# One transformer tower layer on one core: convolution taps from PSUM, a first chain in halves, and a reordered start of the selective scan

## What is computed

```
proj = x @ in_proj.T;  hidden, gate = split(proj)           # 384 channels each
h  = silu(causal_conv4(hidden) + conv_b)                    # depthwise, 4 taps
ts, B, C = split(h @ x_proj.T)                              # 48, 16, 16
dt = softplus(ts @ dt_proj.T + dt_b); dt[last] *= alpha
state = exp(A*dt)*state + dt*B*h;  y = sum_n state*C        # 16 states a channel
out = ((y + h*D) * silu(gate)) @ out_proj.T
```

## Time and profile before

| | us |
|---|---|
| median of three runs (lowest, highest) | 377.47 (377.18, 379.12) |
| the profiled execution, its own time | 380.98 |
| span in its profile | 378.0 |
| TensorE, VectorE, ScalarE, GpSimd busy | 331.5, 243.0, 195.2, 205.5 |

### The profile page before, as it was taken

The page is one execution under the profiler, slowest core; times in us unless marked ns, Lnnn a source line. Parts: engine busy times, 40 slices in busy tenths (PEclk is TensorE's granted clock), DMA queues, the critical chain, the costliest instruction groups (busy, mean ns, idle before and its releaser), DMA issues.

```text
span 378.0 us, 6192 instructions
## 1 busy us (share of the span) xinstructions
PE 331.5 (88%) x1980; PEld 271.4 (72%) x1981; DVE 243.0 (64%) x372; ACT 195.2 (52%) x321; POOL 205.5 (54%) x160
## 2 busy tenths in 40 slices
PE   4898667999987998999798959999999999999960
PEld 3753256867866975688687848888888888888850
DVE  0469789689999899899997966853333222223210
ACT  0126676496994675686925697723233333333310
POOL 2143039898899998898866157500233333333333
PEclk9999855899996799999789696999999999999995
DMA  7990470000023410310999996232233322333222
GB/s 193 273 280 0 148 300 2 0 0 6 2 89 134 151 73 9 105 42 2 195 207 244 290 225 219 86 68 65 53 51 49 49 49 49 49 49 49 21 22 21
DMA packets 30183, 37.00 MB, mean 98 GB/s; under 512 B 6112, under 2 KB 26128, under 8 KB 29136
## 3 DMA queue, kind: packets, MB, share of 16 engines
q1 hardware_dynamic: 23536, 30.54, 29.4%
q0 software_dynamic: 4080, 4.39, 7.7%
q10 hardware_dynamic: 2544, 1.77, 1.9%
HBM read 28.29 MB, written 8.40 MB: 97 GB/s over the span
## 4 chain that ended last, share of the span: by engine, by line
PE 39%; DMA 23%; DVE 15%; issue 11%; ACT 5%; POOL 5%; POOLq 1%; SPq 0%; DVEq 0%; ACTq 0%
DMA out<-ysb,token_r 19%; PE ps L1593 7%; DVE decays L1098 5%; PE ps L1571 5%; POOL states L577 4%; PE ps L1745 3%; PE ps L1427 3%; DMA c_all<-in_xT 3%; PE ps L1432 3%; ACT decays L789 2%; DVE ysb L1319 2%; PE ps L1444 1%; PE ps L1712 1%; DVE xn L974 1%; PE ps L1737 1%
## 5 line engine op out<-in xcount | busy, mean ns | idle before, releaser
L577 POOL TENSOR_TENSOR states<-decays,c_all 128x1024 f32<-128x1024 f32 x48 | 114.2, 2394 | 16.7 <-DVE decays L1098 16.6
L1098 DVE TENSOR_TENSOR_SCAN decays<-decays,ps 128x1024 f32<-128x1024 f32 x48 | 108.1, 2269 | 9.8 <-PE ps L1571 7.3
L679 POOL DMA_INDIRECT out<-ysb,token_r x23 | 36.1, 1570 | 69.1 <-DVE ysb L1319 51.5
L789 ACT ACTIVATE decays<-dt,negA 128x504 f32<-128x504 f32 (+1 forms) x104 | 61.8, 675 | 3.1 <-POOL states L577 3.1
L1593 PE MATMUL ps<-ident,states 128*128 128x128 f32 x384 | 57.3, 296 | 2.5 <-DVE diagB L1021 1.5
L1308 DVE TENSOR_TENSOR hm<-ps,sa 128x512 f32<-128x512 f32 x31 | 21.4, 691 | 55.9 <-PE ps L1718 52.6
L1593 PEld LDWEIGHTS ps<-ident,states 128*128 128x128 f32 x384 | 45.2, 151 | 6.7 <-issue 2.1
L1571 PEld LDWEIGHTS ps<-diagB,stacked_u 64*128 64x128 f32 x384 | 31.8, 207 | 22.1 <-issue 12.6
L1571 PE MATMUL ps<-diagB,stacked_u 64*128 64x128 f32 x384 | 42.3, 318 | 5.9 <-DVE decays L1098 4.6
L901 ACT ACTIVATE sa<-ps 128x512 f32<-128x512 f32 x31 | 18.5, 596 | 55.0 <-PE ps L1718 55.0
L1745 PE MATMUL ps<-w,hT 128*128 (+1 forms) x248 | 45.5, 327 | 0.1
(11 more groups left out here) (195 smaller groups left out, 576.8 us busy)
## 6 DMA issues: line engine op xcount, KB each, us to landing
c_all<-c_scratch SPq DMA_DIRECT2D x8, 1024.0 KB, 4.8
w_raw<-in_w13T SPq DMA_DIRECT2D x9, 512.0 KB, 10.8
w_raw<-in_w13T SPq DMA_DIRECT2D x18, 256.0 KB, 11.3
w<-in_w2T SPq DMA_DIRECT2D x9, 384.0 KB, 15.7
xs<-rows_scratch SPq DMA_DIRECT2D x23, 128.0 KB, 2.4
rows_scratch<-zeros SPq DMA_DIRECT2D x5, 520.0 KB, 6.4
c_all<-in_xT SPq DMA_DIRECT2D x8, 256.0 KB, 10.5
out<-h SPq DMA_DIRECT2D x1, 576.0 KB, 3.5
```

The source lines that it names most:

```text
L577: pool.tensor_tensor(states[:, n % SLOTS, :].rearrange("p (n b s) -> p n b s", n=NH, b=2), decays[:, k % DBUF, t, :, :, :].rearrange("p b ...
L679: pool.indirect_dma_start(out=out_d, out_offset=bass.IndirectOffsetOnAxis(ap=token_r[:, r:r + 1], axis=0), in_=ysb[:, r, :], in_offset=Non ...
L789: return act.activation(decays[:, k % DBUF, tiles[0]:tiles[1], :, n, 1:], dt[g][:, i, tokens].rearrange("p (a b s) -> p a b s", b=2, s=S)[ ...
L1098: dve.tensor_tensor_scan(both, both, unit_banks(n).rearrange("p b n -> p (b n)"), 0.0, ALU.mult, ALU.add).then_inc(scan_ok, 1)
```

## The change

1. Patch products go to six banks (`PATCH_BANK`), so that TensorE waits for VectorE only from tile 6 on; the first transposes come after tile 6 instead of tile 5. VectorE's constants come ahead of the first tile, and the group 1 rows are normalised by ScalarE (`second_rows_normed`, with `less_mean` from GpSimd).
2. `hp` and its zero columns are gone. ScalarE's `projected` writes the projection times the last tap plus the bias into `hid`, and VectorE's `tap` adds the other three taps straight from the PSUM bank, over 63, 62 and 61 columns of each image.
3. Group 1's projections are no longer in front of the scans: `project_first(3)` and `project_second(3)` stand within the first chain, projection 4 after unit 1, projection 5 after units 2 and 3. Their convolutions stand in VectorE's list after scans 0, 3 and 4. A bank is free for the next product when its taps are done (`conv_ok` in place of `hidden_ok`).
4. The chain of z = 0 goes in halves of 256 tokens, from `first_linear` to `first_inputs`, and its copies in `first_copies` by tiles of 128.
5. GpSimd builds `spread_u` and `spread_b` before its first `inverse_deviation`. It builds two diagonals instead of one before the scans, and u for chunk 1 after unit 2.
6. The loads of `outT`, `gateTa` and `gateTb` go from ScalarE's queue to SyncE's, behind the patches.

```
 for n in range(UNITS):                       # VectorE
     scanned(n)
     if n == 0:
-        first_stacked(1)
-        diagonal(0, BUILT_BY_DVE[2])
+        first_low(1)
+        convolved(1, 0)
     if n == 1:
-        u_low_part(1)
+        rest_stacked()
+        diagonal(0, BUILT_BY_DVE[2])
     if n == 2:
+        time_step(0, 1)
         diagonal(0, BUILT_BY_DVE[3])
-    if n == 5:
+    if n == 3:
+        convolved(1, 1)
+    if n == 4:
+        u_low_part(1)
+        convolved(1, 2)
+    if n == 6:
         time_step(0, 2)
...
+def tap(g, i, d):
+    out = hid[g][:, i, :].rearrange("p (b s) -> p b s", b=GB)[:, :, d:]
+    source = ps[:, PROJ_BANK[IC * g + i], :].rearrange("p (b s) -> p b s", b=GB)[:, :, 0:S - d]
+    return dve.scalar_tensor_tensor(out, source, par[:, i, P_CW + K - 1 - d:P_CW + K - d], out,
+                                    ALU.mult, ALU.add)
...
 def projected(n):                            # ScalarE
-        act.activation(hp[:, g, m, :, K - 1:],
-                       ps[:, PROJ_BANK[n], :].rearrange("p (b s) -> p b s", b=GB),
-                       ACT.Copy).then_inc(hidden_ok, 1)
+        act.activation(hid[g][:, m, :], ps[:, PROJ_BANK[n], :], ACT.Identity,
+                       bias=par[:, m, P_CB:P_CB + 1],
+                       scale=par[:, m, P_CW + K - 1:P_CW + K]).then_inc(hidden_ok, 1)
...
-PROJ_BANK = [4, 5, 6, 7, 4, 5, 6, 5, 7, 4, 7, 4]
+PROJ_BANK = [4, 5, 6, 7, 7, 5, 6, 5, 7, 4, 7, 4]
+PATCH_BANK = [0, 1, 4, 5, 6, 7, 0, 1]
...
-PROJ_FREE = {4: 1, 5: 2, 7: 3}
+PROJ_FREE = {3: IC, 4: IC + 1, 5: IC}
...
+            if n in PROJ_FREE:
+                pe.wait_ge(conv_ok, PROJ_FREE[n])
...
 def u_copies(z, half):                       # TensorE
     elif z == 1:
         pe.wait_ge(stacked_ok, 2)
+        pe.wait_ge(conv_ok, G * IC)
...
+def first_copies():
+    pe.wait_ge(half_high, 1)
+    pe.wait_ge(conv_ok, IC)
+    for a in range(2):
+        for low in range(2):
+            if low and a:
+                inputs(0)
+            if low:
+                pe.wait_ge(half_low, 1)
...
-    if n in (1, 10, 21, 25, 34):
-        u_transposes((1, 10, 21, 25, 34).index(n) + 1)
+    if n in (4, 10, 21, 25, 34):
+        u_transposes((4, 10, 21, 25, 34).index(n) + 1)
...
-    if n in (3, 13, 22, 28, 37):
-        u_copies((3, 13, 22, 28, 37).index(n) + 1, 0)
+    if n in (5, 13, 22, 28, 37):
+        u_copies((5, 13, 22, 28, 37).index(n) + 1, 0)
+    if n == 1:
+        project(IC + 1)
     if n == 2:
+        project_first(2 * IC - 1)
+    if n == 3:
+        project_second(2 * IC - 1)
         time_step_product(0, 2)
```

More of the change, by code:

```diff
@@ L629, in _ @@
             pool.tensor_scalar(spread_b[:, :, 128:], source[:, :, 0, :], 0.0, None, ALU.mult).then_inc(copies_ok, 1)
+            for g in range(G):
+                inverse_deviation(pool, chain, g)
             pool.wait_ge(diagonal_ok, 1)
@@ L998, in _ @@
                               0.0, None, ALU.is_gt)
+            dve.wait_ge(ident_ok, 2)
+            dve.tensor_reduce(on_diagonal[:, :], ident[:, :].rearrange("p (q t) -> p t q", t=BLOCK), AX.X,
+                              ALU.add).then_inc(diagonal_ok, 1)
+            dve.wait_ge(ld_pos, 48)
+            chain(dve.tensor_tensor(posb[:, :], posb[:, :], projb[:, :], ALU.add))
+            for t in range(TPG):
+                embedded(t)
+                if t:
+                    statistics(t - 1, h0_ok)
+            moments(0, h0_ok)
+            embedded(TPG)
+            normed(0)
+            for t in range(TPG + 1, TT):
+                embedded(t)
+                statistics(t - 1, h0_ok)
+            moments(1, h0_ok)
             dve.wait_ge(ld_par, 48)
@@ L1513, in u_copies @@
             def u_copies(z, half):
-                if half:
+                if z and half:
                     pe.wait_ge(stacked_ok, 2 * z + 1)
@@ L1532, in u_copies, with first_transposes @@
                                      skip_group_check=True)
[L1533 to L1552 removed]
+                last.then_inc(stack_mm, 1 if z else 2)
+            def first_transposes(half):
+                if half:
+                    pe.wait_ge(u_ok, 1)
+                    pe.wait_ge(first_ok, 1)
+                else:
+                    pe.wait_ge(half_u, 1)
+                for q in range(2):
+                    tokens = slice(HALF * half + 128 * q, HALF * half + 128 * (q + 1))
+                    last = pe.matmul(first_u(half)[:, 128 * q:128 * (q + 1)], u[:, 0, tokens], ident[:, :],
+                                     start=(q == 0), stop=True, is_transpose=True, skip_group_check=True)
+                last.then_inc(uT_mm if half else half_uT, 1)
+            def first_copies():
[7 more added lines that the diff above has]
+                            pe.wait_ge(half_low, 1)
+                        for j in range(BLOCKS):
+                            last = pe.matmul(ps[:, 5 + a, 128 * j:128 * (j + 1)],
+                                             spread_u[:, j, 0:128] if low else spread_u[:, j, 2 * BLOCK:],
+                                             u_low[:, 128 * a:128 * (a + 1)] if low else
+                                             u_high[:, 0, 128 * a:128 * (a + 1)],
+                                             start=(not low and j == 0), stop=True, skip_group_check=True)
+                    last.then_inc(first_mm, 1)
             def inputs(n):
@@ L1576, in inputs @@
                 last.then_inc(dbu_mm, 1)
+            pe.wait_ge(xnT_ok, 2)
+            pe.wait_ge(ld_par, 48)
+            pe.wait_ge(h0_ok, TPG + 1)
+            for n in range(IC):
+                project(n)
+            transposes(1)
+            pe.wait_ge(ld_mid, 32)
+            pe.wait_ge(h0_ok, TT)
+            for i in range(IC):
+                coefficients(0, i)
+            pe.wait_ge(xnT_ok, 2 * G)
+            project_first(3)
+            time_step_product(0, 0)
+            b_transposes(0)
+            project_second(3)
+            b_copies(0)
+            first_transposes(0)
+            first_copies()
+            time_step_product(0, 1)
+            first_transposes(1)
             def summed(n):
```

277 lines of the change are left out of this document (156 added, 121 removed).

## The result

| | before | after |
|---|---|---|
| median, same chip | 378.30 us | 384.92 us |
| ratio, 95% interval | | 1.0174 (1.0117 to 1.0231) |
| the profiled execution, its span | 380.98, 378.0 us | 387.68, 385.9 us |

Slower by 6.6 us; 3.0 were forecast, and 384.9 lies outside the range of 375.2 to 383.0.

What follows compares the result with a forecast made beforehand. VectorE's list of work was taken to pace the scans. Queue waits spend the first scan's lead: unit 16 3.2 us late, less 0.2 regained, is +3.0 on 377.47, giving 380.5 us; range 375.2 to 383.0.

Steps and rivals of the forecast that it cites:

- first scan: End of the halved first chain: the first scan starts at 44.5 against 54.40 us, a lead of 9.9.
- (a): First in-scan convolution waits from 47.8 for ScalarE's copy behind decays; unit 1 at 53.8 us, lead 4.5.
- (b): Next projection stands ahead of unit 2's products on TensorE, at half clock; unit 2 at 59.3 us, lead 1.8.
- (c): Units 2 to 5: chunk 1's decays wait for projection copies; unit 4 at 67.9, unit 5 at 73.1, lead -1.7.
- (d): Third convolution holds chunk 1's stacking banks, delaying decays; unit 8 2.9 us late, unit 16 3.2 late.
- Taps from PSUM: Convolution taps reading PSUM on VectorE: taken as 0.75 us each, between bounds of 0.67 and 0.85.
- second rival: Most of the loss is made up again in idle time from 110 to 190 us: 378.5 us; chance 24%.
- the third: Rival: VectorE's own list, not the queues, sets the pace; unit 8 at 78.5, total 375.4 us; chance 13%.
- I take half from 40 to 62 us: TensorE's granted clock assumed half in that stretch; never falling gives unit 8 at 81.3, half to 70 gives 85.8.
- The clock rival: TensorE's clock stays half to 70 us, unit 8 2.3 us later still: 382.8 us; chance 10%.
- TensorE's list is dense from 53.8 on: The prediction's argument against the clock staying half to 70 us, a case given 10%.
- VectorE beside GpSimd: Chunk 1's time step, moved into the scans beside GpSimd's multiplications: 0 to 0.4 us more, taken as 0.

Runs made afterwards that it cites:

- a2: The changed kernel measured again, no edit; ratio to the kernel before 1.0153.
- a15: The changed kernel measured again, no edit, on another chip than a2; ratio to the kernel before 1.0142.
- e1: The changed kernel with ScalarE's copy of the second group's first projection moved ahead of the first 8 decays; ratio to the kernel before 1.0023.
- e7: e6 with the third convolution ahead of u's low parts and the decays of units 8 to 11 around the first stacking copy; ratio 0.9992.
- e13: e12 plus ten TensorE matmuls with unread results in the front, before the first scan; ratio to the kernel before 0.9881.
- e10: The changed kernel plus 25 TensorE matmuls with unread results: ten in front, ten before projection 4, five ahead of unit 3's products; ratio 1.0053.
- e4: The changed kernel with the loads of outT and the two gate parts back in ScalarE's queue; ratio to the kernel before 1.0172.
- e2: e1 with the first in-scan convolution also moved ahead of the stacking of tile 1, before the first scan; ratio to the kernel before 1.0018.
- e6: e1 with ScalarE copying projection 5 behind the decays of units 4 to 7, not in their middle; ratio to the kernel before 1.0048.
- e8: e7 with both halves of projection 5 together ahead of unit 3's products, plus five matmuls with unread results; ratio to the kernel before 1.0038.
- e3: The changed kernel plus nine 512-column matmuls with unread results in TensorE's wait before projection 4; ratio to the kernel before 1.0112.
- e12: e7 with the second group's first convolution between VectorE's two stacking copies, no added matmuls; ratio to the kernel before 0.9974.
- e5: The kernel before with only the change's front: six patch banks, early selectors, constants first, second rows normed on ScalarE; ratio 0.9932.

## Why the prediction was right in direction and short in size

The position of each unit behind the first scan is what the order decides, so I take the forecast's steps by that (the change's profile).

| step | forecast | measured |
|---|---|---|
| first projection | 21.8 | 21.8 (a2: 21.3, a15: 21.0) |
| coefficient copy | 33.5 | 34.9 (a2: 33.5, a15: 34.1) |
| first scan | 44.5 | 47.4 (a2: 45.2, a15: 46.6) |
| (a) unit 1, behind the first scan | 9.3 | 9.0 |
| (b) unit 2 | 14.8 | 14.3 |
| (c) unit 4 | 23.4 | 25.2 |
| (d) unit 8 | 39.0 | 41.2 |
| unit 16 | 61.1 | 63.5 |
| unit 16 to the end of the span | 275.4 | 275.0 |

**Right.** Taps from PSUM at 0.75 (three take 2.27). VectorE's wait for ScalarE's copy, 3 to 4 us (3.39); e1 takes it away and unit 1 follows at 5.5 us. Unit 2 waits for TensorE. Unit 8's releaser is ScalarE's decays; e7 takes these away. No loss is made up behind unit 16 within the scans, so the second rival falls. VectorE's own list never set the pace here, so the third falls too. It would have: in e13, with the queues mended and the clock up, the lag is 30.7, and VectorE's list, by the forecast's own rows 24.7 from unit 1, is then most of the 27.9 us from unit 1 to unit 8. The 4.6 us that it took as saved for VectorE are 3.5 by the page.

**Wrong: "I take half from 40 to 62 us".** It was 40 to 74 in the change's profile, 38 to 72 in a2's and 39 to 76 in a15's. This is the mis-sized term behind step (c): the wait for projection 5 was put at 3.3 us (61.3 to 64.6) and was 5.50, and unit 4 slid by 1.8 us, unit 8 by 2.2. e10 is the test. Its clock is up from 52 but for 59 to 63, so it is about what I took from 62 on. It has its first scan at 44.4 us, unit 4 23.4 and unit 8 39.2 us behind it, where 44.5, 23.4 and 39.0 were forecast, and its ratio of 1.0053 is 2.0 us of loss on 378.3, for 3.0 forecast. The clock rival, at 10%, had this mechanism: it put the end at 70 and unit 8 at 85.8, that is 41.3 us behind the first scan, and 41.2 was measured. Its sum, 382.8, is 2.1 us short of the median; the first scan's lateness, told below, is left out of it.

The argument against it, "TensorE's list is dense from 53.8 on", was true and did not help. The projection began at 56.47, late by no more than the first scan was, and was followed by work with 0.68 us of waiting in it; the clock took 17 us from there, where I had given it 8. Standing before that projection is a part of it: with ScalarE's copy late (the change, a2, a15, e4) the clock first came back at 72 to 76, with the copy early (e1, e2, e6, e7, e8) at 52 to 68. It is not the whole: e1 and e7 have the same order up to the copy of projection 4 and TensorE busy throughout from 48 to 52 us, and the clock first came back at 68 in one and at 52 in the other. What decides between them stays open. The Trainium skill ("TensorE: Matmul & The Clock Gate", section "What's actually happening") has it that the slow clock is the default and activity lifts it. The trace agrees with the first half (0.50 at 54 to 56 with TensorE at 0.00 busy); for the second, it was busy for 17 us before 0.98 came at 74 to 76. I had named this rule and then priced the late return at a tenth.

**Not foreseen: the clock falls in the front already, or not.** In the change's profile the third coefficient product took 1.91 us for 1.11, in the stretch of 0.78 and 0.50 at 32 to 36. Among the kernels with the change's front and no fills in it the first scan starts at 46.6 to 47.4 where that happened (change, a15, e3, e2 with its convolution ahead) and at 44.6 to 45.5 where it did not (a2, e4, e1, e6, e7, e8, e12). It is the same program both times. The forecast's 44.5 was the best case; the change's three profiles are 0.7 to 2.9 us later. Together, in the change's profile: 3.0 forecast, 2.9 in the front, 2.4 by unit 16, -0.4 behind, gives the 7.9 us of the span. In the medians it is 6.6, and the 2.4 by unit 16 are the part that all three profiles of the change have (2.4 to 2.6).

**VectorE beside GpSimd** was taken at 0, and is: the time step within the scans took 0.67 at 63.90 and at 82.97. GpSimd paid instead; its multiplications of states that began during these two took longer than the others:

```profile
64.06 2.72 POOL L600 TENSOR_TENSOR states<-decays,c_all 128x1024 f32<-128x1024 f32 x1 [2.01 <-DVE decays L1184]
...
68.25 2.36 POOL L600 TENSOR_TENSOR states<-decays,c_all 128x1024 f32<-128x1024 f32 x1
```

By the rule of the Trainium skill ("SBUF — State Buffer", section "SBUF: two separate sides") one locks the other out for the whole instruction. Here the later one took 0.36 us longer, where 0.51 of VectorE's 0.67 were left; a hold to its end would have shown 0.51. The 2.4 us more in the sum, which the prediction drew from that rule, did not come.

**Causes, shown and open.** Shown by taking them away: the copy behind eight decays (1.5% of ratio, e1), all three queue waits together (1.6%, from 1.0153 to 0.9992, e7), and the clock with the queues as they are (1.0%, e10). They are not a sum: ten of e10's fills stand in the very wait that e1 takes away. Open is why the clock falls, and comes back, at different times in executions of one program, what e5's 0.7% consists of, and how e10's gain splits between the front and the scans.

## What to carry to other kernels

Where work moves into a pipelined stage, follow each operand back to the queue in which its producer stands: a copy of 0.8 us behind eight decays cost 3.4 us of the bounding engine. Mend the order first and look at the clock after. Ten idle matmuls in TensorE's short waits were worth 0.9% in the mended order and nothing clear of noise in the other. Do not size such fills by one profile: e8's were sized by e7's, and in e8's own profile TensorE did not stand there. A forecast that needs the slow clock to end at a certain time should carry that time as a range: within the one order of the change it ended at 72, 74 and 76 us.

## What the runs showed of the hardware

The same program had its granted clock fall at 33 us in one profile and not before 38 in another (a15: 0.55 in 32 to 34; a2: 1.00 until 38), worth 1.4 us at the first scan. TensorE at half clock stayed there through long busy stretches: from 56.5 us on it was busy nearly throughout in the change, and the clock came back only at 74; in e1 it was busy throughout from 48 to 58 us, and the clock came back at 68. The later stages have such falls too, in different places in each profile (0.58 in 116 to 120 us in a2, where a15 has 1.00), and spans of one program differ by 1 to 2 us: a2, on another chip than a15, has unit 16 1.4 us earlier and ends 1.2 us later. Under 1%, a single profile ranks nothing; medians do.
